# Two-layer graph network, one core: who increments the semaphore behind TensorE's products in the prepare stage and the first edge loop

## The reference, cut to what matters

```
layer 0, per edge e:  emb = 8 gaussians of the edge's length
                      h = silu(silu(emb @ w0 + b0) @ w1 + b1);  w = h @ w2 + b2      # 4 x 32
                      m = products of w with the sender's (projected) features and the edge's direction
         x = layernorm(x + segment_sum(m, receivers) @ W_out / ...)
layer 1, per edge e:  hidden = relu([x[src], x[dst]] @ W1[type] + b1[type]);  score = sigmoid(...)
                      m = (hidden @ W2[type] + b2[type]) * score
         x = layernorm(x + layernorm(GRU(sum of m per node, x) + x))
```

## Time and profile before

| what | us |
| --- | --- |
| device time, three runs | 2176.5, 2179.9, 2180.6; median 2179.9 |
| span of the profiled execution | 2978.9 |
| PE busy in that span | 2086.4 (70%) |
| DVE busy | 1473.7 (49%) |
| ACT busy | 1324.2 (44%) |
| POOL busy | 1608.3 (54%) |
| mean granted TensorE clock | 0.78 of full |
| first gather starts, in the profile | 29.8 |
| last gather of layer 0, first of layer 1 | 1509.5, 1547.4 |
| last gather of layer 1 | 2944.2 |

### The profile page before, as it was taken

How to read it: one execution, slowest core, us unless ns; L and a number is a source line. 1 busy time by engine, 2 the same in 40 slices (tenths; PEclk the granted TensorE clock), 3 DMA queues, 4 the chain that set the end, 5 groups by cost and what they waited for, 6 DMA issues and landing times. The chain is left out here.

```text
span 2978.9 us, 43422 instructions
## 1 busy us (share of the span) xinstructions
PE 2086.4 (70%) x9981; PEld 1613.0 (54%) x9981; DVE 1473.7 (49%) x3717; ACT 1324.2 (44%) x4373; POOL 1608.3 (54%) x1698
## 2 busy tenths in 40 slices
PE   5777778878787888878775665666655566565566
PEld 3555556555555555556554555555555456555555
DVE  6336344434333434443353444666565656566566
ACT  5445465545555555555432333333333334333343
POOL 6456445555555555555535545456555655555553
PEclk7678788877878887887876777777787777787778
DMA  7211112212222222222235543334343333333332
GB/s 253 60 39 46 48 46 65 54 52 59 57 54 58 54 56 58 56 55 60 55 98 139 141 130 84 90 83 95 83 94 86 91 89 87 91 88 85 91 87 55
DMA packets 220028, 236.10 MB, mean 79 GB/s; under 512 B 72845, under 2 KB 162745, under 8 KB 219548
## 3 DMA queue, kind: packets, MB, share of 16 engines
q0 software_dynamic: 53744, 112.66, 16.4%
q10 hardware_dynamic: 87968, 56.13, 7.5%
q1 hardware_dynamic: 78267, 66.78, 7.4%
HBM read 190.83 MB, written 44.57 MB: 79 GB/s over the span
## 5 line engine op out<-in xcount | busy, mean ns | idle before, releaser
L639 POOL DMA_INDIRECT gx<-node_d,idx x831 | 803.3, 967 | 686.4 <-DVEq L1269 351.9
L639 POOL DMA_INDIRECT gp<-p_tab_d,idx x831 | 788.3, 949 | 646.4 <-DVEq L2188 297.0
L994 PEld LDWEIGHTS ps_a<-hot,msg 128*128 128x128 f32 x3324 | 498.3, 234 | 261.2 <-issue 226.8
L994 PE MATMUL ps_a<-hot,msg 128*128 128x128 f32 x3324 | 530.0, 324 | 90.3 <-issue 36.1
L723 ACT ACTIVATE msg<-ws,y 128x32 f32<-128x32 f32 x2448 | 540.3, 311 | 20.9 <-DVE ws L699 13.5
L1999 PE MATMUL ps_e<-win,hot_x 128*128 128x129 f32 x1664 | 323.9, 368 | 185.5 <-issue 92.9
L1999 PEld LDWEIGHTS ps_e<-win,hot_x 128*128 128x128 f32 x1664 | 297.2, 273 | 215.4 <-issue 114.7
L699 DVE TENSOR_TENSOR ws<-ps_w,gx 128x256 f32<-128x256 f32 (+1 forms) x105 | 44.1, 420 | 633.4 <-remote 530.3
L2088 PE MATMUL ps_g<-hot,hid 128*128 128x128 f32 x1664 | 238.5, 295 | 109.6 <-issue 106.8
L681 PE MATMUL ps_w<-w,h 128*128 128x256 f32 x832 | 265.9, 466 | 33.5 <-issue 33.3
L2088 PEld LDWEIGHTS ps_g<-hot,hid 128*128 128x128 f32 x1664 | 230.5, 211 | 108.3 <-issue 101.2
(11 more groups left out here) (295 smaller groups left out, 2514.6 us busy)
## 6 DMA issues: line engine op xcount, KB each, us to landing
win<-q_tab_d ACTq DMA_DIRECT2D x408, 64.5 KB
key_row<-key_row_d ACTq DMA_DIRECT2D x100, 256.0 KB
gx<-node_d,idx POOLq DMA_INDIRECT x831
gp<-p_tab_d,idx POOLq DMA_INDIRECT x831
p_tab_d<-acc SPq DMA_DIRECT2D x23, 516.0 KB
q_tab_d<-unit_area SPq DMA_DIRECT2D x36, 258.0 KB
q_tab_d<-acc SPq DMA_DIRECT2D x5, 774.0 KB
emb<-emb_d SPq DMA_DIRECT2D x102, 32.0 KB
```

Of the source, the lines that this page charges most:

```text
L639: e.indirect_dma_start(out=buf[:, h, t, :], out_offset=None, in_=table, in_offset=bass.IndirectOffsetOnAxis(ap=idx[:, h, t:t + 1], axis=0) ...
L994: last = e.matmul(ps_a[:, h, b, :], msgs[h].tile(t, b), hot[:, h, t, :], start=t == tiles.start, stop=t == tiles.stop - 1)
```

## The change

In `prepare` and in `edges0` the increment is taken off the last product of a group and put on a `drain` instruction behind it: in both shared helpers (`layer0_second`, `layer0_third`), in `first`, `half_table`, `nodes_out`, `nodes_t` and behind `sums(h, 1)` of a step. `drain` is an instruction of TensorE's sequencer. Left as they were are the products of `node_rows`, `widen` and `first` in `prepare`, the calls `end_sums`, `end_turn` and `last_components` at the end of `edges0`, the count of hits, and all of `edges1`. The products, their order and all waits stay.

```diff
 def layer0_second(e, w, mlp, value):
     e.wait_ge(mlp["h1_ok"], value)
-    e.matmul(mlp["ps_h"][:], w["w1"][:], mlp["h1"][:], start=True, stop=True).then_inc(mlp["h2_mm"], 1)
+    e.matmul(mlp["ps_h"][:], w["w1"][:], mlp["h1"][:], start=True, stop=True)
+    e.drain().then_inc(mlp["h2_mm"], 1)
...
-    layer0_mlp3(e, w, mlp["h2"], mlp["ps_w"][:, h]).then_inc(mlp["w_mm"], 1)
+    layer0_mlp3(e, w, mlp["h2"], mlp["ps_w"][:, h])
+    e.drain().then_inc(mlp["w_mm"], 1)
...
-                    e.matmul(ps_h[:], w["w0"][:], emb[:, h, :], start=True, stop=True).then_inc(h1_mm, 1)
+                    e.matmul(ps_h[:], w["w0"][:], emb[:, h, :], start=True, stop=True)
+                    e.drain().then_inc(h1_mm, 1)
...
-                    e.matmul(to[:, 0:HW], nodes, v["w_p"][:, some], start=b == 0, stop=True).then_inc(p_mm, 1)
+                    e.matmul(to[:, 0:HW], nodes, v["w_p"][:, some], start=b == 0, stop=True)
+                    e.drain().then_inc(p_mm, 1)
...
-                        last = node_sums(v["sums"][:, :, t * P:(t + 1) * P], ps_x[:, t * P:(t + 1) * P])
-                    last.then_inc(o_mm, 1)
+                        node_sums(v["sums"][:, :, t * P:(t + 1) * P], ps_x[:, t * P:(t + 1) * P])
+                    e.drain().then_inc(o_mm, 1)
...
-                        last = e.transpose(ps_x[:, t * P:(t + 1) * P], v["x1"][:, t, :], k["ident"][:])
-                    last.then_inc(t_mm, 1)
+                        e.transpose(ps_x[:, t * P:(t + 1) * P], v["x1"][:, t, :], k["ident"][:])
+                    e.drain().then_inc(t_mm, 1)
...
-                        sums(h, 1).then_inc(sum_mm, 1)
+                        sums(h, 1)
+                        e.drain().then_inc(sum_mm, 1)
```

## The result

The changed kernel takes 2370.9 us (median of six runs, 2359.8 to 2373.2), the kernel before 2180.2 us beside it (six runs, 2176.5 to 2183.3): a ratio of 1.0857 [1.0839, 1.0874]. It is slower by 191 us. 2290 us had been forecast, with a range up to 2350: the direction was right, the size was not.

The account below looks back on a forecast made before the run. GpSimd's gathers were taken as the bound at 40.0 us per iteration. Drains bring TensorE from 36.6 to 44.9 us, +4.9 over 22.5 iterations is +110, plus 2 between the layers: 2290 us from 2179.9, range 2200 to 2350.

Parts of the forecast that it names:

- The bound before: Both layers' loops: GpSimd issues gathers end to end, 1.25 us each, 40.0 us per iteration; rebuilt total 2177.5 us.
- The reading of the 799 us: Profile span 2978.9 us against timed 2179.9: the 799 us belong to the profile itself, not to the timed execution.
- The price of a drain: TensorE in layer 0's loop: 0.39 us where groups flowed on, 0.20 elsewhere, plus sequencer work; 8.3 us per iteration.
- The iteration before: TensorE's iteration with node work in layer 0, summed from four undisturbed steps: 36.6 us, 3.4 under GpSimd's 40.0.
- ScalarE and VectorE don't decide: Layer 0's steps: their waits ahead of TensorE have slack in undisturbed steps, and longer steps give them more.
- The clock: Rival, chance 0.06: new gaps lower TensorE's clock in layer 0 to a mean of 0.80, +317, about 2500 us.
- all new gaps as 0.2 to 0.4 us: TensorE's stream behind each drain: new gaps of 0.2 to 0.4 us, against clock falls following idle stretches of several us.
- A low clock in steps without a long wait: Sign in the changed kernel's profile by which the prediction said it would be wrong.
- The three iterations without node work: Layer 0's loop: TensorE goes from 32.5 to 38.5 us each, still under 40.0, so no cost.
- Between the layers: Nine half tables in a chain, whose drains give increments later and hold the next product: 0 to 3 us, taken as 2.
- A nearly free drain: Rival, chance 0.11: loads and products pass on during a drain, under 0.15 us each in TensorE's slack; 2180 us.
- a gain from late releases: Rival, chance 0.06: increments on products come late in timed runs, on drains at once; 2133 us from 47 per iteration.

Follow-up runs that it names:

- experiment 7: A 0.72 us operation on GpSimd ahead of each layer 0 step's gathers: 2266.4 us added to the kernel before, 2363.6 us added to the changed kernel.
- experiment 3: The kernel before with only the drain behind `layer0_second`, four per iteration: 2176.0 us, ratio 0.9985 to the kernel before.
- experiment 2: The changed kernel without the drains of the node work, 16 per iteration instead of 22: 2262.1 us, ratio 1.0375 to the kernel before.
- experiment 4: The changed kernel without the drain of `first` in u = 3, ahead of the back edge, 21 per iteration: 2286.7 us, ratio 1.051 to the kernel before.
- experiment 9: The changed kernel with drains only behind `layer0_second`, `layer0_third` and `sums(h, 1)`, 12 per iteration: 2216.9 us, ratio 1.0184 to the kernel before.
- experiment 8: The kernel before with drains only in `prepare`, the three iterations without node work and the half tables at the end: 2185.6 us, ratio 1.0042.
- experiment 5: The changed kernel without the drain of `first` in u = 1, the back edge's kept, 21 per iteration: 2356.4 us, ratio 1.0785 to the kernel before.
- experiment 1: The changed kernel with increments back on the products and drains that carry nothing left behind them: 2360.4 us, ratio 1.0821 to the kernel before.

## Why the prediction was right, and where it failed

**The bound before** held. GpSimd's gathers set the pace at 40.0 us an iteration: experiment 7 added 0.72 us of work 96 times and lost 85.5 us, and experiment 3 shows gathers from end to end. The sum of 2177.5 us, from a trace of 2978.9, met the measured 2180.2, but that is luck. In experiment 3's trace on the first kind of chip the 2 x 831 gathers take 1056.4 + 1043.4 = 2099.8 us and not 2077.6 (layer 0's have pauses and longer single gathers that the median hides), and the passage between the layers and the end take 20.7 + 27.6 us and not 36.6 + 33.5. One error is 22 us too little, the other 22 too much.

**The reading of the 799 us** failed, and should not be hidden by that hit. The prediction said that they "belong to the profile itself". They don't: device time is the span plus some 2.1 us in each run (2359.8 and 2357.6; 2991.2 and 2989.1). They belong to the chip on which the trace was taken. The same reading gave the sentence that the changed kernel's span would say little on its time; it gave the time within 2.2 us.

**The price of a drain** held for the changed kernel: 9.62 us for a step u = 1 (9.3 to 9.7 forecast), 0.40 us behind the stream's end (0.4), 44.8 us for an iteration (44.9), 22 iterations at +112 us (+110). Experiments 2, 4 and 9 put the points between. But the start of this sum was wrong. The iteration before was put at 36.6 us from four steps of a disturbed trace, and "ScalarE and VectorE don't decide" left out the wait for ScalarE in u = 2: it takes 38.06 us (experiment 8). That 44.8 fits 44.9 all the same is owed to the drains of u = 2, behind which this wait disappears, and that is luck too. The step u = 3 was read 0.23 us too long as well (9.64 against 9.41), since its first row is a slowed one, 0.83 us instead of 0.60. One where the next group flowed on costs 0.47 (experiment 3; 0.46 forecast), one where rows change 0.26 (9.62 against 9.36 for u = 1 in experiment 9; 0.27 forecast). Only the back edge's is dearer: 0.63 us an iteration (44.80 against 44.17 in experiment 4) where 0.47 had been counted.

**The clock** is the term that failed: +56 us where the forecast's sum counted nothing, together with the reason for counting nothing. It was weighed as a rival and given 0.06, against it that falls in the trace follow idle stretches of several us. The trace of before does not bear that out for every fall. The very stretch of the earlier trace rows lies in one that began at 943.1 us: the array was dense until 940.7, then 0.97 us idle, had one product, and was idle for 1.1 us more when the clock fell:

```profile
941.66 0.38 PE L681 MATMUL ps_w<-w,h 128*128 128x256 f32 x1 [0.97 <-issue]
943.78 0.59 PE L681 MATMUL ps_w<-w,h 128*128 128x256 f32 x1 [1.74 <-issue]
```

```profile
930.00:943.00 13.00, 11.06 (x61) 7.97 (x61) 2.45 (x6) 4.60 (x18) 9.95 (x11) 1.00 0.20 50
943.20:963.50 20.30, 14.01 (x41) 9.12 (x40) 9.56 (x22) 12.49 (x42) 8.88 (x10) 0.50 0.13 33
```

Nor was the rival right as it stood: it took a mean clock of 0.80 and 2500 us; the loop had 0.94. The second half of the failed step is the one that took all new gaps as 0.2 to 0.4 us. At the back edge, drain, branch and waits add up to 0.70 us, and experiments 4 and 5 show 70 us of difference between losing that gap and losing another. A low clock in steps without a long wait was one of the signs by which the prediction said it would be wrong, and that sign came. Why such a gap is followed by a fall in 17 of 20 cases here and in 7 of 20 in experiment 2 stays open. The Trainium skill, TensorE: Matmul & The Clock Gate, section "A second HAM failure mode: psum-queue depth-cycling", says that short idle times between groups can make the clock swing; the traces agree in that (0.70 us ahead of a fall to 0.50), but not for every gap: with 21 drains and gaps of 0.21 to 0.33 us an iteration it fell twice in 22 iterations (experiment 4), with 12 drains not once (experiment 9).

**The three iterations without node work** were counted at nothing, because 38.5 us lie under 40.0. Undisturbed they do (38.8 us in experiment 1, 39.0 in experiment 8, with the same 16 drains). But the cover was gone: once TensorE bounds the loop behind them, each microsecond it is late at its start stays. In experiment 3 the second of them runs at 34.4 us and makes up for a late start; in the changed kernel it takes 40.2. Measured +11 us.

**Between the layers** 2 us were forecast for the drains; from TensorE's last L681 it is 3. Gathers see 11, because TensorE's last step now begins 6.9 us behind the start of the last gather instead of 1.0 ahead of it. That belongs to the changed bound.

**The rivals.** A nearly free drain and a gain from late releases are both out: experiment 3 shows the price even where the time does not move, and on chips with late releases the change is slower by 162 us. With the 112 + 56 + 11 + 1 us (the last is +3 and -2 of the table), 2180 becomes 2360, the profiled run; the median run is 11 us above that, and the share of the clock in those 11 was not traced.

## What to carry to other kernels

A drain behind a group costs TensorE the run-out of its array, its sequencer's bare work and the lost prefetch of weights, 0.26 to 0.47 us here for the three together (the runs do not price them apart) and 0.63 at the back edge, although it is one instruction. What the kernel pays is what remains above the engine that bounds it: four of them nothing, twelve 40 us, twenty-two 191. When a change makes another engine the bound, go back to every edit that was "hidden" and price it again, loop entries and back edges too; and look for the place at which several small bare times meet, since there TensorE's clock can fall, which here cost half as much as the drains themselves. A sum that meets the measured time is no proof of its terms: here two errors of 22 us cancelled. Before a slow trace is explained, check its own device time against its span: it may be another chip.

## What the runs showed of the hardware that was not expected

- Two kinds of chips: the same kernel takes 2177 to 2181 us on the one kind, and 2931 and 2980 us on two chips of the other. On the slow ones VectorE starts 4.2 us (median) behind the last product that it waits for, against 0.04 us, and drains end late instead where they carry the release. TensorE's products also pause inside a group there, as by 0.97 and 1.74 us in the rows above. Why was not found.
- With an idle gap of 0.70 us once per iteration TensorE is at half its clock for 126 us of the loop; with 21 gaps of 0.21 to 0.33 us alone for 7 us. Six drains fewer elsewhere in the iteration, at the same gap of 0.70 us, left 31 us of it, and doubling all drains 68 us, so it isn't a matter of idle time in sum, nor of the one gap alone.
- A second drain behind a drain costs 0.08 us, against 0.26 to 0.63 for the first.
- A low clock in a loop that another engine bounds costs nothing: 147 us at half the clock in the slowed kernel before, in whose layer 0 no gather waits for VectorE.
